# A new order of the unit's steps and of the opening in a 4-bit feed-forward kernel on one core

## The chip, the cores and the metric

One NeuronCore of a Trainium2 chip. Times are device microseconds of one execution of the whole kernel. Five engines run their own instruction streams and meet at semaphores: TensorE (PE, matmuls; PEld is its weight loading), VectorE (DVE), ScalarE (ACT), GpSimd (POOL) and SyncE (SP, which issues the DMAs).

## The reference

For `x` of 4 x 512 x 512 in float32 the kernel computes

```
xn  = layernorm(x)                              # over the last axis
y   = causal_convolution(xn, K) + D * xn        # K: a kernel of 512 taps from the S4 parameters
g, u = xn @ Wg.T, xn @ Wu.T                     # Wg, Wu: 1792 x 512
out = x + y + (silu(g) * u) @ Wd.T              # Wd: 512 x 1792
W   = NF4_CODE[q] * absmax                      # each weight: a 4-bit code, one scale per 64 codes
```

There are 2048 tokens (16 tiles of 128), 512 features and 1792 inner features (14 tiles of 128, `NM`). All three weight matrices come as int32 codes and block scales and have to be turned into numbers on the chip.

## The kernel before

**Numbers.** Each float32 operand of a matmul is split in two float16 halves, high and low, and each product is three matmuls (high by high, high by low, low by high).

**Units.** A unit is a 128 x 512 tile of weights; there are 42: gate and up of each of the 14 inner tiles, and 14 of the down matrix. Making one takes: the codes by DMA; `first_pass` on POOL (line 845) for one side of the code table, and a chain of six passes on ACT (line 936); on DVE `step(u, WHOLE)` (line 1309), which joins the sides, and `step(u, SCALED)` (line 1313), which multiplies by the scales; the high half, `weight_hi(u)`, on ACT (line 963) for the first seven units and on POOL (line 858) from the eighth on; the low half, `weight_lo(u)`, on DVE (line 1323), which waits for the high half. Behind `SCALED` of an up unit DVE makes two sums for the blocked products (`up_sums`, lines 1347 and 1349), POOL copies a gate unit (`gate_copy`, line 867), and DVE makes two more sums (`other_sums`, lines 1357 and 1360), whose halves are `block_hi` on ACT (1057) and `block_lo` on DVE (1369, 1372).

**Stages.** 1. The opening (to about 33 us): the norms of the x tiles (`stats`, `moments`, `rstd` in twelve small steps on DVE; the normalising on ACT for tile 0 and on POOL, line 749, for the others), the common scales (`scales`), the transposes of tiles 0 to 7 on PE (`turn`, line 2145), their halves (`x_hi` on ACT, line 1095; `x_lo` on DVE, line 1551), and the first products (line 2109). 2. Gate and up products of inner tiles 0 to 2 for all four token groups of 512, in the order of `OPENING`. 3. A window for each inner tile from 3 to 13. Windows 3 and 4 are mixed; from 5 on both halves of the tokens go by a scheme with seven block products instead of eight, `blocked_product` (line 2264), for each of two sides s. On PE a window is: product 1 of both sides, product 4 of the tile before, then 5, 6, 2, 3 and 7 of both sides. DVE adds them up in joins (line 1412): product 3 waits for the side's first join, product 4 for its second. The output of gate and up goes through silu on ACT (line 1020), a multiplication on DVE (`h_mul`, line 1438), and the halves of h (`h_hi`, on POOL line 827, and `h_lo`, line 1450). 4. The convolution as Toeplitz matmuls (line 2331), from about 297 us; the down products (lines 2341 and 2391) to the end. The S4 kernel's own small steps (line 1798 and around) lie between the items of windows 7, 8 and 10 to 13 as a `stage` called behind each slot.

**What sets the order.** Each engine's list is written out by hand. In a window the items of the units (three for each unit on DVE) are dealt over eight slots by `eighths`: with two units per window slots 1, 2, 3 and 5, 6, 7 hold one item each, with three units slots 0 to 6 hold one each and slot 7 two. `EARLY_IN` says which inner tiles' windows make a down unit as well as their two, so that they have three; the last window, 13, has three in any case. From window 6 on `window(k)` on DVE runs: second join, `h_mul(n + 3)`, second join of the other side, `h_mul(n + 1)`, `block_lo(k, 1)`, `h_mul(n + 2)`, slots 0 and 1, `h_mul(n)`, slots 2 and 3, the first join of side 0, slot 4, `h_lo`, slot 5, the first join of side 1, slots 6 and 7, `other_sums(k + 1)`, `block_lo(k + 1, 0)`. On ACT, `copy_m1(1, k)` (line 1029) waits for `h_mul(n)`, and side 1's product 6 for that copy. On POOL each unit u from 7 on is, in this order: `first_pass(u + 2)`, which waits for `step(u, WHOLE)`; `h_hi` of the tile before, if u is a window's first unit; `weight_hi(u)`, which waits for `step(u, SCALED)`; `gate_copy(u)`.

In the opening PE runs two groups of matmuls with the identity whose results nothing reads (`warm_up`, line 2130): ten before the first transpose of x and six behind the fourth.

## Time and profile before

| | |
|---|---|
| time, median of 3 runs | 459.99 us (459.29 to 460.63) |
| the profiled execution: time, span | 460.08 us, 458.3 us |
| PE matmul busy | 438.2 us (96%), 2560 matmuls |
| PE weight load busy | 248.8 us (54%) |
| DVE busy | 398.4 us (87%) |
| ACT busy | 278.8 us (61%) |
| POOL busy | 214.6 us (47%) |
| chain that ended last | PE 85%, DVE 6%, ACT 2%, issue 2%, DMA 2%, POOL 1% |

An engine's busy time is what its instructions cover; overlapping instructions of one engine count once. A row of a timeline gives the start, the length, the engine, the line, what is written and read, how many instructions it merges, and in brackets how long the engine stood before it and what it waited for. The length is that of one instruction from its start to its end; in a dense row the next one starts some 0.08 us before the last one's end, so a DVE step of 0.68 takes 0.60 of the engine's time.

### The profile page before, as it was taken

How to read it: one execution, taken by the hardware profiler on the slowest of the kernel's cores; microseconds unless marked ns; L12 is line 12 of the kernel's file. 1: busy time of each engine (PE TensorE's matmuls, PEld its weight loads, DVE VectorE, ACT ScalarE, POOL GpSimd, SP SyncE). 2: the span in 40 equal slices, each digit the busy share in tenths (PEclk: the TensorE clock that was granted, in tenths of full speed). 3: DMA queues.
4: the chain of work that ended last, by engine and by line, in shares of the span. 5: the costliest groups of instructions: out<-in, count | busy, mean ns of one | idle time of the engine just before them, and what ended most of it. 6: DMA issues, size and time to landing. Idle time of an engine off the chain costs nothing.

```text
span 458.3 us, 7272 instructions
## 1 busy us (share of the span) xinstructions
PE 438.2 (96%) x2560; PEld 248.8 (54%) x2560; DVE 398.4 (87%) x641; ACT 278.8 (61%) x472; POOL 214.6 (47%) x163
## 2 busy tenths in 40 slices
PE   1879999999999999999999999999999999999997
PEld 1534444443444444434444444466544788888886
DVE  5988979969889798999897879879996999999993
ACT  7868594295877759588684787856032542445340
POOL 2777299547456848669646847778100000000000
PEclk9989999999999999999999999999999999999999
DMA  8543636022315415155222233457691021101111
GB/s 291 172 131 139 144 75 182 1 92 71 138 47 183 161 47 200 54 183 191 63 69 65 61 80 101 111 187 249 193 369 60 1 94 47 46 1 48 47 47 46
DMA packets 34168, 51.41 MB, mean 112 GB/s; under 512 B 13076, under 2 KB 14164, under 8 KB 33364
## 3 DMA queue, kind: packets, MB, share of 16 engines
q1 hardware_dynamic: 34132, 50.95, 35.3%
q8 instruction: 20, 0.33, 0.3%
q14 instruction: 16, 0.13, 0.1%
HBM read 38.03 MB, written 10.81 MB: 107 GB/s over the span
## 4 chain that ended last, share of the span: by engine, by line
PE 85%; DVE 6%; ACT 2%; issue 2%; DMA 2%; POOL 1%; SPq 0%; DVEq 0%; ACTq 0%; POOLq 0%
PE bank L2264 33%; PE bank L2391 21%; PE bank L2109 16%; PE bank L2341 8%; PE bank L2331 6%; ACT work L936 1%; DMA h<-in_x 1%; DVE h L1438 1%; DVE work L1313 1%; DMA work<-in_q_gate 1%; DVE w L1323 1%; DVE work L1309 1%; PE bank L2145 0%; DVE h L1412 0%; POOL h L845 0%
## 5 line engine op out<-in xcount | busy, mean ns | idle before, releaser
L936 ACT ACTIVATE work<-work 128x512 f32<-128x512 f32 (+1 forms) x234 | 130.0, 628 | 11.5 <-POOL work L845 7.8
L845 POOL TENSOR_SCALAR work<-work 128x512 f32<-128x512 int32 x39 | 85.9, 2202 | 64.4 <-DVE work L1309 46.1
L2264 PE MATMUL bank<-h 128*128 128x512 f16 x360 | 81.5, 379 | 0.9 <-ACT bank L1029 0.9
L2109 PE MATMUL bank<-xT,w 128*128 128x512 f16 (+1 forms) x300 | 66.2, 377 | 2.3 <-DVE w L1323 1.1
L2264 PEld LDWEIGHTS bank<-h 128*128 128x128 f16 x360 | 34.9, 98 | 44.0 <-ACT bank L1029 2.4
L2391 PE MATMUL bank<-wd,work 128*128 128x256 f16 x504 | 56.2, 273 | 0.0
L2264 PE MATMUL bank<-xT,w 128*128 128x512 f16 x240 | 55.4, 379 | 0.0
L2391 PEld LDWEIGHTS bank<-wd,work 128*128 128x128 f16 (+1 forms) x504 | 49.3, 98 | 6.0
L2109 PEld LDWEIGHTS bank<-xT,w 128*128 128x128 f16 x300 | 29.4, 99 | 36.8 <-DVE w L1323 2.4
L1250 ACT ACTIVATE work<-h 128x896 f16<-128x896 f32 x30 | 27.9, 942 | 28.4 <-DVE h L2017 18.3
L2391 PE MATMUL bank<-h,work 128*128 128x256 f16 x378 | 42.2, 273 | 0.0
L858 POOL TENSOR_SCALAR w<-work,sc 128x512 f16<-128x512 f32 x21 | 39.0, 1857 | 6.6 <-DVE work L1313 5.6
L2391 PEld LDWEIGHTS bank<-h,work 128*128 128x128 f16 x378 | 37.0, 98 | 4.3
L2264 PEld LDWEIGHTS bank<-xT,w 128*128 128x128 f16 x240 | 23.4, 98 | 28.1
L2341 PE MATMUL bank<-wd,h 128*128 128x512 f16 x168 | 36.4, 379 | 0.0
L1309 DVE SCALAR_TENSOR_TENSOR work<-work 128x512 f32<-128x512 f32 x39 | 28.4, 729 | 5.1 <-ACT work L936 5.1
L2003 DVE TENSOR_TENSOR work<-h,work 128x896 bf16<-128x896 f32 x30 | 32.5, 1083 | 0.1
L1313 DVE SCALAR_TENSOR_TENSOR work<-work 128x512 f32<-128x512 f32 x41 | 29.9, 730 | 1.5
L1029 ACT ACTIVATE bank<-bank 128x512 f32<-128x512 f32 x20 | 11.6, 582 | 31.7 <-DVE work L1438 15.6
L1020 ACT ACTIVATE work<-bank,sc 128x512 f32<-128x512 f32 x36 | 24.6, 684 | 9.9 <-PE bank L2109 9.9
L2264 PE MATMUL bank<-xT,h 128*128 128x512 f16 x120 | 28.1, 379 | 1.2 <-DVE bank L1412 1.0
L858 POOL TENSOR_SCALAR wd<-work,sc 128x512 f16<-128x512 f32 x14 | 26.3, 1877 | 4.7 <-DVE work L1313 3.8
(181 smaller groups left out, 672.0 us busy)
## 6 DMA issues: line engine op xcount, KB each, us to landing
moved<-h SPq DMA_DIRECT2D x6, 1024.0 KB, 4.9
h<-moved SPq DMA_DIRECT2D x4, 1536.0 KB, 15.5
h<-in_x SPq DMA_DIRECT2D x8, 512.0 KB, 5.4
xT<-in_x SPq DMA_DIRECT2D x16, 256.0 KB, 3.5
out<-xT SPq DMA_DIRECT2D x15, 256.0 KB, 2.1
work<-in_q_gate SPq DMA_DIRECT2D x14, 256.0 KB, 3.6
work<-in_q_up SPq DMA_DIRECT2D x14, 256.0 KB, 2.9
work<-in_am_gate SPq DMA_DIRECT2D x28, 128.0 KB, 3.1
```

Of the source, the lines that this page charges most:

```text
L845: pool.tensor_scalar(chain_room(u, "r"), qs[:, u % 2, :], RIGHT_FROM, RIGHT_FROM, ALU.max, ALU.subtract).then_inc(first_done, 1)
L858: pool.tensor_scalar(weight_of(u)[HI], whole_of(u), scale_of(u), None, ALU.mult).then_inc(phi_done, 1)
L936: nc.scalar.activation(room, qs[:, u % 2, :] if j == 0 else room, KNEE, scale=scale, bias=bias, alpha=below).then_inc(knee_done, 1)
L1250: nc.scalar.activation(slot_of(o)[:, HI], src, ACT.Copy).then_inc(o_hi, 1)
L1309: ins = v.scalar_tensor_tensor(whole, left, CHAIN_TOP if u in CHAINED else LEFT_TOP, right, ALU.min, ALU.add)
L1313: ins = v.scalar_tensor_tensor(whole, whole, CHAIN_STEP if u in CHAINED else -LEFT_TOP, am[:, u % 2, :], ALU.add, ALU.mult)
L2003: v.tensor_tensor(slot[:, LO].bitcast(BF16), src, slot[:, HI], ALU.subtract).then_inc(o_lo, 1)
L2109: mm = nc.tensor.matmul(out_b, weights(k)[:, unit, wl, f, :], xT[:, TPC * c + first:TPC * c + last, xl, f, :], start=(i == 0), stop=(i == ...
L2264: mm = nc.tensor.matmul(out_b, weight(wl, f), token(xl, f), start=(n == 0 and i in (1, 5)), stop=(n == 5), skip_group_check=i not in (1, 5))
L2331: mm = nc.tensor.matmul(bank[(t + 4) % 8][:, P * j:HD], xT[:, t, xl, j, :], tz[:, tl, 0:HD - P * j], start=(n == 0), stop=(n == 3 * NC - 1))
L2341: mm = nc.tensor.matmul(bank[(t + 4) % 8][:], part, wd[:, mt, wl, :], start=(mt == 0 and n == 0), stop=(mt == NM - 1 and n == 2))
L2391: mm = nc.tensor.matmul(out_b, part, w, start=(n == 0), stop=(n == 3 * KT - 1))
```

## The change

Six edits. (1) `EARLY_IN` goes from (7, 8, 9, 11) to (6, 7, 9, 12). (2) On DVE each unit's three items come in the order low half of the unit before, whole, scaled; before it was whole, scaled, low half of the unit before. (3) In the windows from 6 on `h_mul(n)` comes behind slot 0 instead of behind slot 1. (4) The two groups of unread identity products are gone, and the product that spreads the common scales comes ahead of `turn(0)`. (5) In the opening the steps of the norms, scales, first units and transposes come in another order on SP, POOL, ACT, DVE and PE. (6) On PE `products(1, (0,))` comes ahead of `turn(4)`. The same work is done otherwise.

```diff
--- before.py
+++ after.py
@@ -119,7 +119,7 @@
 
 
 
-EARLY_IN = (7, 8, 9, 11)
+EARLY_IN = (6, 7, 9, 12)
 EARLY = len(EARLY_IN)
 SEQ = list(range(9))
 for k in range(3, NM - 1):
@@ -662,11 +662,11 @@
             load_x(1)
             load_codes(1, q_up[0])
             sp.dma_start(amf, am_flat).then_inc(amf_ld, 16)
-            load_x(2)
-            load_x(3)
             load_absmax(0, am_gate[0])
             load_codes(2, q_gate[1])
+            load_x(2)
             load_absmax(1, am_up[0])
+            load_x(3)
             load_codes(3, q_up[1])
             load_absmax(2, am_gate[1])
             sp.dma_start(cols[:], s4_cols).then_inc(s4_ld, 16)
@@ -871,9 +871,9 @@
                 norm(t)
             first_pass(2)
             first_pass(3)
-            first_pass(4)
             for t in range(TPC, 2 * TPC):
                 norm(t)
+            first_pass(4)
             first_pass(5)
             for i in range(14):
                 v_step(i)
@@ -1100,10 +1100,10 @@
             chain(1, 0, 5)
             norm(0)
             chain(1, 5, 6)
+            chain(2, 0, 1)
+            weight_hi(0)
             x_hi(0)
-            weight_hi(0)
             x_hi(1)
-            chain(2, 0, 1)
             x_hi(2)
             x_hi(3)
             chain(2, 1, 2)
@@ -1111,17 +1111,16 @@
             chain(2, 2, 6)
             chain(3, 0, 2)
             weight_hi(2)
-            chain(3, 2, 4)
+            chain(3, 2, 6)
+            silu(0)
+            act.wait_ge(b_mm, 1)
+            nc.scalar.activation(yv[:, 0:2], bank[3][:, 0:2], ACT.Copy).then_inc(b_cp, 1)
+            weight_hi(3)
             x_hi(4)
-            chain(3, 4, 6)
-            silu(0)
-            chain(4, 0, 1)
-            weight_hi(3)
             x_hi(5)
             x_hi(6)
-            act.wait_ge(b_mm, 1)
-            nc.scalar.activation(yv[:, 0:2], bank[3][:, 0:2], ACT.Copy).then_inc(b_cp, 1)
             x_hi(7)
+            chain(4, 0, 1)
             chain(4, 1, 6)
             h_hi(0)
             silu(1)
@@ -1327,7 +1326,7 @@
                 for p in range(first, last):
                     u, i = item_of(DVE_AT, p)
                     if u in CHAINED:
-                        i = (3, 4, 2)[i]
+                        i = (2, 3, 4)[i]
                     if i != 2:
                         step(u, i if i < 2 else i - 1)
                     elif u > 0:
@@ -1566,27 +1565,27 @@
             rstd(0, 3)
             rstd(0, 4)
             rstd(0, 5)
-            step(0, WHOLE)
+            scales(1)
             rstd(0, 6)
             rstd(0, 7)
             rstd(0, 8)
-            scales(1)
+            scales(2)
             rstd(0, 9)
-            scales(2)
+            scales(3)
             rstd(0, 10)
-            scales(3)
+            scales(4)
             rstd(0, 11)
-            scales(4)
             dve.wait_ge(id_done, 1)
             scales(5)
+            scales(6)
+            step(0, WHOLE)
+            step(0, SCALED)
             stats(4)
-            scales(6)
-            step(0, SCALED)
-            step(1, WHOLE)
             scales(7)
             scales(8)
+            step(1, WHOLE)
+            weight_lo(0)
             x_lo(0)
-            weight_lo(0)
             x_lo(1)
             step(1, SCALED)
             x_lo(2)
@@ -1596,31 +1595,31 @@
             stats(6)
             stats(7)
             moments(4, 8)
+            step(2, WHOLE)
             rstd(1, 0)
             rstd(1, 1)
             rstd(1, 2)
-            scales(9)
+            step(2, SCALED)
             rstd(1, 3)
             rstd(1, 4)
             rstd(1, 5)
-            step(2, WHOLE)
+            scales(9)
             rstd(1, 6)
             rstd(1, 7)
             rstd(1, 8)
-            step(2, SCALED)
+            weight_lo(2)
             rstd(1, 9)
+            scales(10)
             rstd(1, 10)
+            scales(11)
             rstd(1, 11)
-            weight_lo(2)
             stats(8)
-            x_lo(4)
-            scales(10)
             step(3, WHOLE)
-            scales(11)
+            scales(12)
             step(3, SCALED)
             h_mul(0)
-            scales(12)
             weight_lo(3)
+            x_lo(4)
             x_lo(5)
             x_lo(6)
             stats(9)
@@ -1763,9 +1762,9 @@
                     h_mul(n + 1)
                     block_lo(k, 1)
                     h_mul(n + 2)
-                    stage_of(0, 2)
+                    stage_of(0, 1)
                     h_mul(n)
-                    stage_of(2, 4)
+                    stage_of(1, 4)
                     join(0, k, 0)
                     stage_of(4, 5)
                     h_lo(n)
@@ -2145,15 +2144,14 @@
                     mm = nc.tensor.transpose(bank[4 + t % TPC][:, P * f:P * f + P], xnb[:, t, P * f:P * f + P], ident[:])
                 mm.then_inc(tp_done, 1)
 
-            warm_up(10)
-            turn(0)
             pe.wait_ge(one_done, 1)
             pe.wait_ge(sc_done, 7)
             nc.tensor.matmul(bank[0][:, P:P + 6], ones[:], dg3, start=True, stop=True).then_inc(mx_bc, 1)
+            turn(0)
             turn(1)
             turn(2)
             turn(3)
-            warm_up(6)
+
 
             pe.wait_ge(wlo_done, 1)
             pe.wait_ge(xlo_done, 2)
@@ -2165,8 +2163,8 @@
             for i in range(2):
                 mm = nc.tensor.matmul(bank[3][:, i:i + 1], vcs[:, P * i:P * i + P], bps, start=True, stop=True)
             mm.then_inc(b_mm, 1)
+            products(1, (0,))
             turn(4)
-            products(1, (0,))
             turn(5)
             turn(6)
             turn(7)
```

## Rows read from the trace of the kernel before

**Rows 1.** The page: the span, and the x loads among the DMA issues

```profile
span 458.3 us, 7272 instructions
...
h<-in_x SPq DMA_DIRECT2D x8, 512.0 KB, 5.4
```

**Rows 2.** Waits of TensorE: engine, line, releaser: total us, times, longest

```profile
PE bank L2145 <- POOL h L749: 2.9, 1, 2.9
PE bank L2109 <- DVE w L1323: 1.1, 1, 1.1
PE bank L2264 <- DVE bank L1412: 1.0, 1, 1.0
PE bank L2264 <- ACT bank L1029: 0.9, 1, 0.9
```

**Rows 3.** Timeline, TensorE, 0 to 40: start, us, engine line op out<-in xcount

```profile
9.81 2.34 PE L2130 MATMUL bank<-ident 128*128 128x256 f16 x10
...
17.13 1.47 PE L2109 MATMUL bank<-xT,w 128*128 128x256 f16 x12 [0.62 <-DVE xT L1551]
...
26.88 4.45 PE L2109 MATMUL bank<-xT,w 128*128 128x512 f16 x12
...
33.01 7.30 PE L2109 MATMUL bank<-xT,w 128*128 128x512 f16 x33 [0.37 <-ACT yv L1123]
```

**Rows 4.** Busy time by stretch: five engines, then the granted clock, DMA, GB/s

```profile
28.00:32.00 4.00, 4.00 (x17) 1.95 (x16) 3.56 (x8) 2.79 (x6) 3.23 (x3) 0.66 0.00 1
```

**Rows 5.** Timeline, VectorE, 0 to 60, the same columns

```profile
25.74 1.09 DVE L1323 SCALAR_TENSOR_TENSOR w<-work,sc,w 128x512 f16<-128x512 f32 x1 [0.32 <-ACT w L963]
...
34.24 0.68 DVE L1551 TENSOR_TENSOR xT<-bank,xT 128x512 f16<-128x512 f32 x1
...
47.62 0.73 DVE L1323 SCALAR_TENSOR_TENSOR h<-work,sc,h 128x512 f16<-128x512 f32 x1
```

**Rows 6.** Timeline, ScalarE, 0 to 60

```profile
24.98 0.72 ACT L963 ACTIVATE w<-work,sc 128x512 f16<-128x512 f32 x1 [3.10 <-DVE work L1313]
...
33.31 3.15 ACT L936 ACTIVATE h<-h 128x512 f32<-128x512 f32 x5
```

**Rows 7.** Timeline, GpSimd, 0 to 70

```profile
25.52 3.45 POOL L749 TENSOR_SCALAR h<-h 128x512 f32<-128x512 f32 x4 [1.40 <-DVE h L1544]
```

**Rows 8.** Timeline, VectorE, 60 to 130

```profile
110.80 1.09 DVE L1323 SCALAR_TENSOR_TENSOR w<-work,sc,w 128x512 f16<-128x512 f32 x1
```

**Rows 9.** Timeline, VectorE, 200 to 300, in tile 9's and tile 11's windows

```profile
205.11 0.68 DVE L1309 SCALAR_TENSOR_TENSOR work<-work 128x512 f32<-128x512 f32 x1
...
207.26 0.47 DVE L1349 SCALAR_TENSOR_TENSOR h<-work,sc,h 128x256 f32<-128x256 f32 x1
...
211.80 1.09 DVE L1323 SCALAR_TENSOR_TENSOR w<-work,sc,w 128x512 f16<-128x512 f32 x1
...
251.76 0.75 DVE L1323 SCALAR_TENSOR_TENSOR w<-work,sc,w 128x512 f16<-128x512 f32 x1 [1.39 <-POOL w L858]
```

**Rows 10.** Timeline, GpSimd, 200 to 300, first unit of tile 10's window

```profile
224.72 1.93 POOL L845 TENSOR_SCALAR work<-work 128x512 f32<-128x512 int32 x1 [3.41 <-DVE work L1309]
226.71 0.61 POOL L827 CAST h<-work 128x512 f16<-128x512 f32 x1
227.29 2.01 POOL L858 TENSOR_SCALAR w<-work,sc 128x512 f16<-128x512 f32 x1
```

**Rows 11.** Timeline, TensorE, 130 to 200: first products of tile 6, its product 3

```profile
143.04 2.75 PE L2264 MATMUL bank<-xT,w 128*128 128x512 f16 x12
...
155.99 2.75 PE L2264 MATMUL bank<-xT,h 128*128 128x512 f16 x12
```

**Rows 12.** Timeline, VectorE, 130 to 200: the first join in tile 6's window

```profile
144.59 0.68 DVE L1412 TENSOR_TENSOR h<-bank,h 128x512 f32<-128x512 f32 x1
```

**Rows 13.** Timeline, VectorE, 200 to 300, in tile 13's window

```profile
289.22 0.91 DVE L1798 TENSOR_SCALAR wd<-wd,sc 128x512 f16<-128x512 f32 x1
...
294.40 0.69 DVE L1412 TENSOR_TENSOR h<-bank,h 128x512 f32<-128x512 f32 x1 [0.60 <-PE bank L2264]
```

## The prediction

> **What bounds the kernel now.** I read the busy times first: TensorE (PE) is busy nearly throughout the 458.3 us span [rows 1]. Then its waits [rows 2], leaving out the 9.7 us before its first instruction, which the change doesn't shorten: 2.9 us in the opening, 1.1 us on a low half (line 1323) at the end of tile 3's window, and 1.0 and 0.9 us in tile 8's window, on a join and on the copy behind the last `h_mul`. Everywhere else PE sets the pace. A wait that goes is gained whole if no other takes its place; a delay of VectorE (DVE) costs nothing until it eats the slack before the product that asks for its result. Third, the timelines of DVE and GpSimd (POOL), for that slack.
>
> **The opening.** The 16 unread identity products go: ten take 2.34 us [rows 3], all in waits, so they free no time on the critical path. `step(0, WHOLE)` (0.6) leaves the chain of small steps, but the first product still waits for `weight_lo(0)`, then two `x_lo`: by my count of the new order 17.0 against 17.13 [rows 3]. No gain there.
> The second tile's gate product is where the order bites. It now starts at 26.88, behind `turn(4)`; its low half, begun at 25.74 [rows 5], had waited for ScalarE (ACT), which had stood 3.1 us for `step(2, SCALED)` [rows 6]. In the new order DVE ends the moments at 21.6, W(2) at 22.2, three small steps at 22.6, S(2) at 23.2; ACT's high half takes 0.7, and the low half runs 24.3 to 25.0. (W, S, L: the whole, scaled and low-half steps of a unit.) The product doesn't wait for a transpose any more and starts at 25.0, 1.9 earlier. Its twelve matmuls took 4.45 us [rows 3], with a granted clock of 0.66 over 28 to 32 [rows 4], the lower level (1.2 GHz) for most of it, after a wait of 2.9. Twelve at the upper level take 2.6 (0.216 each in the dense stretches). The idle time ahead of it is now 1.6 at most, so I take 2.6: end 27.6. The norms of x tiles 4 to 7 still start with the last small step, at 25.6 against 25.52 [rows 7], and end 29.1; the last transpose is done 29.7, `products(1, (1,))` 32.3, and the last `x_lo`, now at 34.24 [rows 5], ends at 32.4. Products of the third pair start at 32.4 against 35.6 (33.01 [rows 3] and twelve of 0.216): 3.2 earlier.
> Not all of it lasts. Fifteen products later PE asks for the low half of unit 5: now at 48.5, when that half (47.62 plus 0.73) is just done [rows 5]. ACT's fourth chain, now over at 36.46 [rows 6], ends at 34.4 (`x_hi(7)` at 30.6 and six passes of 0.63), and DVE is behind it all the way, so unit 5 is ready 2.2 earlier. I count **-2.3**.
> SP: x tiles 4 to 7 go behind two scale loads and the codes of unit 2, whose issue waits for the first knees (5.4); with 5.4 us to land [rows 1] and a start near 6.1 the first is there at 11.6, and `stats(4)` asks at 13. It costs nothing; a late one would delay the scales, and with them all weights, by as much. The other moves of POOL (`first_pass(4)` behind the norms, ends 31.0, first asked for at 32.5) and ACT cost nothing either.
>
> **Tile 3's window.** L(9), now last [rows 8], comes right behind the second join, so PE's 1.1 us wait [rows 2] goes: **-1.1**. In tile 4's window the next low half waits for POOL some 1.6 us, inside DVE's own wait of 1.2 for PE and a join slack of 1.7: 0.
>
> **The blocked windows.** Before, a unit's three items come as W(u), S(u), L(u-1); after, as L(u-1), W(u), S(u). So L(u) follows S(u) as the next item, where W(u+1) and S(u+1) had lain between. L(u) needs the high half from POOL, and POOL's queue behind W(u) is `first_pass(u+2)`, 1.93, then `h_hi` 0.61 at a window's first unit, then `weight_hi(u)`, 2.01, 1.6 with DVE quiet [rows 10]: from the end of W(u) to the high half **4.4** us at a first unit, 3.9 at a second. DVE has between them at a first unit in a three-unit window only S (0.7) and the two sums (0.9): W 205.11 to the end of the sums at 207.7 [rows 9]. It stands 2.8 us. At the second unit `h_lo`, S and a join (1.9) lie between: 2.0 more. Before, the same distance held five or more items (W 205.11, the window's first unit's L at 211.8) and cost nothing; where POOL was late, in tile 11's window, L already stood 1.39 [rows 9].
> Behind the stalled L wait, on DVE, the two first joins of the window, and PE's product 3 waits for these. With P as the window's start on PE, product 3 of one side comes at P+12.95 (143.04 to 155.99 [rows 11]), of the other 1.3 later. **Tile 6**, now with three units: DVE starts its first join at P+1.55 [rows 12], is through the three `h_mul` and L(u-1) at P+7.3, W 7.9, sums 9.5; high half 12.4, L 13.0, join 13.65: PE stands 0.75. W, `h_lo`, S, second join 16.1 against 14.25+0.75: 1.15 more. **+1.9**. The third unit ends DVE's window at P+21.5, that is 1.5 after PE's next start, as it entered.
> **Tile 7** the same with 1.7 us of inverse steps in it: joins at P+14.35 and 17.5, PE stands 1.4 and 1.85, less the 0.4 it loses now: **+2.9**. **Tile 8** loses its third unit, and `h_mul(n)` comes before W; both waits there [rows 2] go but 0.3: **-1.7**. **Tile 9** (three units before and after) enters with 1.8 us more slack: **+0.7**. Tiles 10 and 11 have other work of theirs in the gap: 0. **Tile 12** gets a third unit: **+0.7**, and ends 2.8 after PE's start, so PE's product 4 stands **1.0**. **Tile 13**, three units and the kernel's scaling (two steps, the first at 289.22 [rows 13], 1.6 in all): stalls of 3 and 2 us, joins 0.4 and 1.5 late; then DVE comes to the last two joins at P+23.0, 2.1 behind product 7, where now it stands 0.60 for PE [rows 13], and product 4 waits for them: **+4.0**. In the convolution and behind it DVE stalls again (1.0 per unit), which the 4 us of waits for loads and for ACT there cover.
> Sum of the windows +1.9 +2.9 -1.7 +0.7 +0.7 +1.0 +4.0 = +9.5. With -2.3 and -1.1: **+6.1**. The profiled execution took 460.08, 1.8 around its span of 458.3, and the median is 459.99, so they stand for each other: 466.
> Bounds: the high half costs DVE at least nothing (L finds it ready) and at most 4.1 less the 1.6 between, at each unit; VectorE beside a busy POOL stretches single steps from 0.7 to 1.1 [rows 5, 8], which adds up to 0.7 per three-unit window, some 4 in all.
>
> **A rule against the opening's part.** The identity products are also the only long run of ordinary matmuls before 17.13: the first ten ran at 0.234 per 256 columns, the pace of the lower level, and the first product's twelve at 0.123, the upper [rows 3]. What is left before it are transposes. By the Trainium skill ("TensorE: Matmul & The Clock Gate", Part 4: PE-mode transpose) a transpose doesn't count as busy in the same way for the clock. By that rule the rival below on the clock holds; no row here parts transposes from matmuls.
>
> **Rivals.** *DVE has the room (faster).* L finds its high half, or the stalls fit into DVE's idle time. POOL would have to deliver within 1.6 us of W instead of 4.4, or a three-unit window would need 5 us idle on DVE; now they have 1 to 2. For it speak the two-unit windows, with 2.5 us idle, that steps beside a quiet POOL run in 0.7 instead of 1.1, and that the early units leave tile 8, where PE stood. It decides below some 1 us of stall per unit. Then -2.3 -1.1 -2.0 = -5.4: 454.6; with half of the stalls about 460.
> *The clock (slower still).* The first 36 matmuls run at the lower level throughout: 24 of 0.213 and 12 of 0.427 are 10.2 instead of 5.2. They end near 27.9, the next gate product at 30.7, the third pair starts at 35.0: the opening gives 0.6 instead of 2.3, 468. Against it: the transposes fill the time from 12 to 16, and PE has 1.6 us to spare before 25.0.
> *It does nothing.* Gains and stalls cancel: tile 13's last joins cost 1 instead of 4 and the rest 0.5 each; 460.
>
> **Chances.** My forecast 0.53, the clock on top of it 0.09, room on DVE 0.28, nothing 0.10. A measurement of this kernel can tell about 0.3% from no change. Slower 0.62, same 0.09, faster 0.29. The forecast's own range is 462 to 471 (opening -3 to -1, tile 13 +1.5 to +5, port contention up to +4); with the other side it is 455 to 471.
>
> **What would show it.** Right: in the rows after, line 1323 of DVE with waits for POOL of 2 to 3 us in the windows of tiles 6, 7, 9, 12 and 13; PE waits for joins (line 1412) of 8 us or more in all; product 4 of tile 13 late; no wait at 111; the third pair's start at 32 to 33. Wrong: DVE waits for POOL under 1 us each, or PE dense from 33 to 297; or a granted clock at the lower level between 17 and 33, and the opening no shorter.

## The result and the profile after

The changed kernel takes 477.15 us (475.77 to 477.67), the one before 459.64 beside it: a ratio of 1.0377 (95% interval 1.0344 to 1.041), or 17.5 us slower where 6.1 were forecast. The profiled execution has a span of 475.6 us against 458.3 [rows 1], so it has the same difference, 17.3. Lines of the changed kernel are one or two lower than before: W is 1308, S 1312, L 1322, the join 1411, the fourth product of the epilogue 1437.

The page after: the span, busy times, and the chain that ended last.

```profile
span 475.6 us, 7240 instructions
...
PE 439.3 (92%) x2544; PEld 247.2 (52%) x2544; DVE 395.3 (83%) x641; ACT 281.9 (59%) x472; POOL 209.0 (44%) x163
...
PE 58%; DVE 18%; POOL 7%; issue 7%; DMA 5%; ACT 3%; SPq 0%; DVEq 0%; POOLq 0%; ACTq 0%
```

The engines have about the same to do and are busy for a smaller share. The chain was PE for 85% before and is PE for 58% now, with 25% on DVE and POOL (7% before). The waits, of PE, DVE, POOL and ACT (engine, line, releaser: total us, times, longest; against [rows 2]):

```profile
PE bank L2262 <- DVE bank L1411: 11.9, 9, 2.1
...
PE bank L2262 <- DVE h L1411: 3.8, 3, 1.6
...
PE bank L2262 <- DVE h L1368: 0.8, 1, 0.8
```

```profile
DVE wd L1322 <- POOL wd L858: 19.1, 10, 3.3
DVE w L1322 <- POOL w L858: 16.2, 7, 2.9
```

```profile
POOL work L845 <- DVE work L1308: 82.6, 29, 5.8
```

```profile
ACT work L936 <- POOL work L845: 26.2, 19, 1.9
```

L now waits for POOL's high half 17 times, 35.3 us in all; before it did so for 3.3. POOL's `first_pass` in turn waits 82.6 us for W, where it waited 46.1. Two engines that each wait for the other, and neither is full: they take turns. One turn, in tile 7's window, on DVE (172.01 on) and on POOL:

```profile
172.01 0.68 DVE L1308 SCALAR_TENSOR_TENSOR work<-work 128x512 f32<-128x512 f32 x1
...
172.87 0.68 DVE L1312 SCALAR_TENSOR_TENSOR work<-work 128x512 f32<-128x512 f32 x1
173.68 0.62 DVE L1346 TENSOR_TENSOR h<-work 128x256 f32<-128x256 f32 x1
174.22 0.47 DVE L1348 SCALAR_TENSOR_TENSOR h<-work,sc,h 128x256 f32<-128x256 f32 x1
177.59 0.75 DVE L1322 SCALAR_TENSOR_TENSOR w<-work,sc,w 128x512 f16<-128x512 f32 x1 [2.90 <-POOL w L858]
...
179.26 0.68 DVE L1308 SCALAR_TENSOR_TENSOR work<-work 128x512 f32<-128x512 f32 x1
```

```profile
172.84 2.50 POOL L845 TENSOR_SCALAR work<-work 128x512 f32<-128x512 int32 x1 [3.28 <-DVE work L1308]
175.40 0.61 POOL L827 CAST h<-work 128x512 f16<-128x512 f32 x1
175.99 1.57 POOL L858 TENSOR_SCALAR w<-work,sc 128x512 f16<-128x512 f32 x1
180.10 2.23 POOL L845 TENSOR_SCALAR work<-work 128x512 f32<-128x512 int32 x1 [2.54 <-DVE work L1308]
```

W(u) ends at 172.7, POOL needs until 177.56, L(u) stands 2.90 for it, and only behind L comes W(u+1), at 179.26; by then POOL has stood 2.54. The joins lie behind these L: product 3 of tile 7 starts after waits of 1.75 and 2.07 on PE.

Where the 17.3 us lie, from the starts of each window on PE in the two timelines (us; the third column is the window after minus before):

| stretch | before | after | more | forecast |
|---|---|---|---|---|
| to tile 3's start (PE's first instruction came at 9.54 after, 9.65 before) | 87.41 | 86.29 | -1.1 | -2.3 |
| from there to the product that waited for L(9) | 24.54 | 23.31 | -1.2 | -1.1 |
| from there to tile 5's start | 15.55 | 15.54 | 0 | 0 |
| tile 5 | 15.54 | 16.62 | +1.1 | 0 |
| tile 6 | 18.13 | 22.75 | +4.6 | +1.9 |
| tile 7 | 18.49 | 24.02 | +5.5 | +2.9 |
| tile 8 | 20.45 | 19.07 | -1.4 | -1.7 |
| tile 9 | 18.13 | 19.81 | +1.7 | +0.7 |
| tiles 10, 11 | 39.04 | 39.04 | 0 | 0 |
| tile 12 | 18.27 | 19.40 | +1.1 | +0.7 |
| tile 13 | 21.24 | 26.84 | +5.6 | +5.0 |
| convolution | 26.08 | 26.08 | 0 | 0 |
| first part of the down products (line 2339) | 36.26 | 37.66 | +1.4 | 0 |

### The profile page after: what moved, and what is told of

Its sections match the earlier page's. It is cut to its first block, busy times and chain, and to the rows that moved or that the text cites. A ratio compares the mean times of both kernels' runs of the same rounds, so it can differ in the third digit from the quotient of the medians.

```text
span 475.6 us, 7240 instructions
## 1 busy us (share of the span) xinstructions
PE 439.3 (92%) x2544; PEld 247.2 (52%) x2544; DVE 395.3 (83%) x641; ACT 281.9 (59%) x472; POOL 209.0 (44%) x163
## 4 chain that ended last, share of the span: by engine, by line
PE 58%; DVE 18%; POOL 7%; issue 7%; DMA 5%; ACT 3%; SPq 0%; DVEq 0%; POOLq 0%; ACTq 0%
PE bank L2389 20%; PE bank L2262 15%; PE bank L2108 10%; PE bank L2339 7%; PE bank L2329 5%; POOL work L845 3%; DVE work L1308 3%; DMA lines<-wd 3%; DVE work L1312 2%; POOL w L858 2%; DVE w L1322 2%; DVE bank L1411 2%; DVE h L1498 1%; ACT work L936 1%; DMA h<-in_x 1%
## 5 line engine op out<-in xcount | busy, mean ns | idle before, releaser
L936 ACT ACTIVATE work<-work 128x512 f32<-128x512 f32 (+1 forms) x234 | 131.7, 623 | 36.7 <-POOL work L845 26.2
L845 POOL TENSOR_SCALAR work<-work 128x512 f32<-128x512 int32 x39 | 87.3, 2238 | 92.5 <-DVE work L1308 82.6
L2108 PE MATMUL bank<-xT,w 128*128 128x512 f16 (+1 forms) x300 | 64.7, 371 | 3.8 <-DVE w L1322 1.9
L2262 PE MATMUL bank<-xT,h 128*128 128x512 f16 x120 | 29.8, 390 | 11.9 <-DVE bank L1411 11.9
L858 POOL TENSOR_SCALAR w<-work,sc 128x512 f16<-128x512 f32 x21 | 36.0, 1716 | 7.2 <-DVE work L1312 6.0
L1322 DVE SCALAR_TENSOR_TENSOR w<-work,sc,w 128x512 f16<-128x512 f32 x25 | 20.2, 808 | 16.4 <-POOL w L858 16.2
L1312 DVE SCALAR_TENSOR_TENSOR work<-work 128x512 f32<-128x512 f32 x41 | 30.8, 752 | 2.2
L2262 PE MATMUL bank<-h,w 128*128 128x512 f16 x120 | 28.0, 379 | 3.8 <-DVE h L1411 3.8
```

The source lines that it names most:

```text
L845: pool.tensor_scalar(chain_room(u, "r"), qs[:, u % 2, :], RIGHT_FROM, RIGHT_FROM, ALU.max, ALU.subtract).then_inc(first_done, 1)
L858: pool.tensor_scalar(weight_of(u)[HI], whole_of(u), scale_of(u), None, ALU.mult).then_inc(phi_done, 1)
L936: nc.scalar.activation(room, qs[:, u % 2, :] if j == 0 else room, KNEE, scale=scale, bias=bias, alpha=below).then_inc(knee_done, 1)
L1312: ins = v.scalar_tensor_tensor(whole, whole, CHAIN_STEP if u in CHAINED else -LEFT_TOP, am[:, u % 2, :], ALU.add, ALU.mult)
L1322: v.scalar_tensor_tensor(lo, whole_of(u), scale_of(u), hi, ALU.mult, ALU.subtract).then_inc(wlo_done, 1)
L2108: mm = nc.tensor.matmul(out_b, weights(k)[:, unit, wl, f, :], xT[:, TPC * c + first:TPC * c + last, xl, f, :], start=(i == 0), stop=(i == ...
```

## The experiments

Each is given against the kernel before or the changed kernel, and its ratio is to the kernel before, run beside it (459.3 to 459.9 us). In each W, S and L are as in the prediction.

**The parts one by one.** e1: the changed kernel with the old order of a unit's items.

```diff
-                        i = (2, 3, 4)[i]
+                        i = (3, 4, 2)[i]
```

> The changed kernel with the unit's three items back in their old order (whole, scaled, low half of the unit before); the early tiles, the opening, the missing identity products and the earlier h_mul(n) stay. If the new order is the cause of the loss: no waits of VectorE's low half for GpSimd of 2.9 us, nearly no PE waits between 33 and 297 us, and the gains stand alone: 1.1 us measured at the start of tile 3's window and the 1.9 us of tile 8's window, 456 to 458 us, ratio 0.991 to 0.996. If instead the missing identity products, the opening or the new early tiles carry a good part of the loss: above 463 us.

Measured 460.01, ratio 1.0008 (0.9995 to 1.002). L(9) waits its 1.07 again; everything else of the 17 us is gone. e2: the kernel before with the new order alone (the same line the other way).

> The kernel before with one edit: the unit's three items in the new order. If the order is the cause: tile windows 7, 8, 9, 11 and 13 have three units, each stands 2.9 us and 1.9 us at its two low halves; PE loses some 5 us in tile 7, 4 in tile 8 (it had lost 2 before), 1.7 in tile 9, 1 in tile 11, 5.5 in tile 13 and 2 in tile 5, less 1.1 in tile 3: 474 to 480 us. If the order costs only together with the new early tiles: under 466 us.

Measured 471.43, ratio 1.0255 (1.023 to 1.0279): less than I expected. So the order is necessary for the loss, but two thirds of it by itself. e3: the kernel before with the opening's order on all engines and without the identity products; e4: only `EARLY_IN = (6, 7, 9, 12)`.

> The kernel before with the new orders of the opening on all engines and without the identity products; nothing changed in the windows. The changed kernel began tile 3's window 1.1 us earlier. If this gain carries to the end: 458.9 us, ratio 0.9975, third pair of products at 33.7 us. If the windows' own loops take it back: 460 us. If cold matmuls eat it: a granted clock under 1 between 17 and 33 us, and no gain.

> The kernel before with EARLY_IN (6, 7, 9, 12) alone. Under my theory tile 8's window loses its third unit and with it both PE waits (1.9 us), and tiles 6 and 12 have room for one in the old order: 458 us, ratio 0.996, no PE wait in tile 6's window above 0.5 us. Rival: the third unit in tile 6 costs what the one in tile 8 did: 460 us.

Measured: e3 459.08, 0.9981 (0.9966 to 0.9996), a gain of 0.9; e4 460.21, 1.0021 (1.0002 to 1.0039), a loss of 1.0. Both are small: their intervals end just short of no change. In e4 PE waits 0.79 in tile 6, which now has a third unit, and 0.72 in tile 7, which had one before too; both waits are for ACT's bank copy (line 1029), and tile 8's join wait stays at 1.00. These three parts by themselves add up to 11.8, and with the fourth (e10, below) to 13.7, not 17.5, so some of them meet. e7 has order and places together, e9 the changed kernel with `h_mul(n)` back behind slot 1, e10 the move of `h_mul(n)` alone in the kernel before (the "moved product" is this step on DVE):

```diff
-                    stage_of(0, 1)
+                    stage_of(0, 2)
                     h_mul(n)
-                    stage_of(1, 4)
+                    stage_of(2, 4)
```

> The kernel before with two of the four parts: the new order of the items of each unit, and the down units at tiles 6, 7, 9, 12. The order alone cost 11.6 us and the other places alone 1.0, while all parts together cost 17. Theory 1 (the parts meet at these places: two three-unit windows in a row, 6 and 7, with no slack carried between, and a third unit in tile 12 whose lateness tile 13 takes over): 475 to 478 us, with 4.5 or more lost in each of the windows 6 and 7 and 5 in 13. Theory 2 (the meeting is with the opening's new order or the moved product of the epilogue): 471 to 473 us.

> The changed kernel with one part taken back: the epilogue's fourth product (h_mul(n)) stands after the items of the first two eighths of a window again, not after those of the first. Two of the four parts together (order and places of the down units) took 471.2 us, all four 477. Theory 1: the moved product puts the first unit's W or S, and with them GpSimd's halves, one product (0.7 us) later, so the L wait of a window is 2.90 us where it was 2.05, and each three-unit window costs about 1 us more: without it 470.0 to 471.5 us, the first L wait of tile 7 at 2.0 to 2.1 us. Theory 2: it is the opening's order that meets the rest: 476 to 477.5 us.

> The kernel before with only the moved product (h_mul(n) after the first eighth's items). Theory 1 (it costs only where GpSimd's halves are already what L waits for, which in the old order they are not): 459.3 to 460.2 us, ratio 0.999 to 1.002. Theory 2 (it takes about 0.7 us from the second join of each window by itself): 461 to 464 us.

Measured: e7 471.16, 1.0259 (1.023 to 1.0289), the same as the order alone: it is not the places, whose 1.0 us by themselves doesn't show on top of the order. e9 471.70, 1.0256 (1.0229 to 1.0283), against 1.0377 with the moved product: it costs 1.2% or 5.6 us here, where e10 has 1.9. e10 461.75, 1.0042 (1.0025 to 1.0059): 1.9 us in the old order, my second theory: PE's waits for joins are 3.4 us in all against 1.0 [rows 2], in tiles 7, 8, 10 and 11. ACT's wait in tile 8 (0.9) is gone in return. With the product ahead of slot 1, in which W or S of the window's first unit lies, that step comes 0.7 later and POOL's halves with it. In the new order L then stands 2.90 in tile 7, where in e7 and e9 it stands 2.05. Windows 6, 7, 9 and 12 are 21.6, 23.0, 18.6 and 18.2 long in e9 and 22.8, 24.0, 19.8 and 19.4 in the changed kernel: 1.1 to 1.2 in each. The row of e7 (VectorE, tile 7's first unit):

```profile
175.09 0.75 DVE L1323 SCALAR_TENSOR_TENSOR w<-work,sc,w 128x512 f16<-128x512 f32 x1 [2.05 <-POOL w L858]
```

**Is it POOL?** e5: the changed kernel with a shorter `first_pass` from tile 5's units on (7/8 of that side's decoding is left out). e13: the same cut in the kernel before.

```diff
-                pool.tensor_scalar(chain_room(u, "r"), qs[:, u % 2, :], RIGHT_FROM, ...
+                n = CH if u < made_before(5) else 64
+                pool.tensor_scalar(chain_room(u, "r")[:, 0:n], qs[:, u % 2, 0:n], RIGHT_FROM, ...
```

> The changed kernel, with VectorE's new order, in which GpSimd's subtraction of the right half (first_pass) takes 64 of its 512 columns from the fifth tile's units on. The part left out is the decoding of 448 columns of those units, so its time is that of a smaller computation. Theory 1: L(u) waits for GpSimd's two halves of the unit (up to 3.3 us in the changed kernel, 35.3 us in 17 waits), and that wait is what became late for TensorE. With first_pass 1.3 to 1.7 us shorter each wait shrinks by about as much: 35 us of L waits fall to 10 or less, the unit that VectorE finishes last in a window comes in time, and the kernel takes 461 to 468 us. Theory 2: VectorE has simply too much to do in three-unit windows, and its order only moves the place where that shows: L waits fall and the joins wait instead, 473 to 477 us.

> The kernel before, with the same cut as e5_pass_cut: GpSimd's subtraction of the right half takes 64 of 512 columns from the fifth tile's units on; what is left out is the decoding of the other 448 columns. Theory 1 (in the old order L waits 3.3 us for GpSimd in the whole run, so a shorter subtraction gives TensorE nothing): 458 to 460 us, and the 15 us that the cut gave the changed kernel are the order's. Theory 2 (GpSimd's amount of work is a bound of its own): 450 us or less.

Measured: e5 462.08, 1.0063 (1.0042 to 1.0084), 15 us below the changed kernel. e13 459.31, 0.9994 (0.9982 to 1.0005). The same cut gives 15 us in the new order and nothing in the old. So POOL's amount of work is no bound; how soon it delivers is what costs, and only in the new order. Two waits shrink at once in e5, so it doesn't part them: ACT's chain waits 2.3 us for `first_pass` instead of 26.2, and L's waits are:

```profile
DVE wd L1323 <- POOL wd L859: 11.0, 10, 1.8
DVE w L1323 <- POOL w L859: 9.0, 6, 1.7
```

20.0 instead of 35.3 us in all, not the 10 that I expected; with each under 1.9 the joins are nearly in time (PE waits 4.6 us for them instead of 15.7). e6: POOL makes the high half first.

```diff
-                if u + 2 < UNITS:
+                late = u >= made_before(6)
+                if not late and u + 2 < UNITS:
                     first_pass(u + 2)
 ...
                 weight_hi(u)
+                if late and u + 2 < UNITS:
+                    first_pass(u + 2)
```

> The changed kernel, in which GpSimd makes the high half of a unit's weight ahead of the subtraction for the unit two later, for the units from tile 6 on. Theory 1 (L waits for the high half, because it stands behind that subtraction on GpSimd): L waits fall from 2.9 us to 1.2 or less; the subtraction comes about 1.5 us later, and ScalarE's chain, which waits for it, comes later by as much. If ScalarE has the room, 464 to 469 us; if its chain is what then ends last, 474 to 480 us. Theory 2 (VectorE's amount of work alone): 474 to 477 us whatever GpSimd's order.

Measured 475.81, 1.0349 (1.0318 to 1.0381). L's waits fall to 15.7 us (1.7 at most), yet the time stays. The waits of DVE and of ACT in e6:

```profile
DVE h L1371 <- ACT h L1060: 17.8, 8, 3.2
DVE wd L1325 <- POOL wd L858: 8.6, 9, 1.1
```

```profile
ACT work L939 <- POOL work L845: 52.0, 22, 5.3
```

ACT's chain now waits 52.0 us for the late `first_pass` (26.2 before this edit), and `block_lo` 17.8 for ACT. Both of POOL's steps hang on the late W: whichever goes first, someone stands.

**Which exchange?** The new order moves L(u-1) ahead of both W(u) and S(u). e14: the kernel before with L between the two. e16: the changed kernel with the same.

```diff
-                        i = (3, 4, 2)[i]
+                        i = (3, 2, 4)[i]
```

> The kernel before with a third order of a unit's items, W(u), L(u-1), S(u): L stands ahead of S only. Old order (W, S, L) 459.7 us; new order (L, W, S) 471.4. W(u) starts ScalarE's next step and the subtraction two units later; S(u) releases GpSimd's high half. Theory 1 (L's wait costs by how many of the unit's items stand between it and the high half of the unit before, and by how late W and S leave): L(u-1) comes after S(u-1) and W(u) only, its waits are about 0.7 us shorter than in the new order (27 to 30 us in all become 15 to 20), and W(u) isn't late: 463 to 467 us. Theory 2 (what costs is that S(u), and so the high half, comes late): 469 to 472 us. Theory 3 (only W's place matters): 459.5 to 461 us.

> The changed kernel with one exchange: W(u), L(u-1), S(u) in place of L(u-1), W(u), S(u). Theory 1 (the 17 us are W(u)'s place behind L's wait, and the moved product and the places of the down units cost only through it): 458.5 to 460.5 us, L's waits for GpSimd under 10 us in all. Theory 2 (the moved product and two three-unit windows in a row, 6 and 7, cost in this order too, by 2 to 5 us): 461 to 465 us.

Measured: e14 458.03, 0.9973 (0.9958 to 0.9988), faster than any of my three theories allowed, and 13 us faster than e2, from which it differs by the exchange of two neighbouring items, W(u) and L(u-1). L waits for POOL 5.1 us in all (3.6 for gate and up units, 1.5 for down units; 3.3 before), and PE waits 2.2 for joins. The rows of VectorE in tile 7's window, to hold beside those of the changed kernel:

```profile
164.53 0.68 DVE L1309 SCALAR_TENSOR_TENSOR work<-work 128x512 f32<-128x512 f32 x1
...
167.07 0.68 DVE L1313 SCALAR_TENSOR_TENSOR work<-work 128x512 f32<-128x512 f32 x1
...
169.37 0.68 DVE L1309 SCALAR_TENSOR_TENSOR work<-work 128x512 f32<-128x512 f32 x1
...
170.97 0.73 DVE L1323 SCALAR_TENSOR_TENSOR w<-work,sc,w 128x512 f16<-128x512 f32 x1
```

W(u) starts at 164.53, W(u+1) at 169.37 without waiting for anything of POOL's, and L(u), at 170.97, finds its half done: 5.8 us lie between W(u)'s end and L(u), more than the 4.8 that POOL took here. In the changed kernel W(u+1) stands behind L(u), so this distance can't grow. Why S behind L is even a gain is told by the waits of PE: L(9)'s 1.07 and ACT's 0.95 in tile 8 are gone, at 0.55 and 0.6 more at joins (tiles 7 and 8). That is 0.9 net, of the 1.2 measured (0.6 to 1.9 by the interval).

e16 462.24, 1.0045 (1.0021 to 1.0069): 15 of the 17.5 us come back by this exchange alone. By themselves the moved product (+1.9), the places (+1.0), the opening (-0.9) and e14's order (-1.2) would come to +0.8 and not the 2.1 measured (1.0 to 3.2 by the interval). In its profiled execution one L wait of 5.40 us stands out, and PE's 2.05 behind it; tile 13 is 25.1 long there, 21.2 before. POOL's rows say what made it long:

```profile
272.06 1.94 POOL L845 TENSOR_SCALAR work<-work 128x512 f32<-128x512 int32 x1 [4.96 <-DMA work<-in_q_down]
274.09 1.57 POOL L858 TENSOR_SCALAR wd<-work,sc 128x512 f16<-128x512 f32 x1
```

The high half stood behind a `first_pass` that waited 4.96 for the codes of a down unit. The kernel before has such a wait too (5.34, at 274.23), but no L that waits behind it. So in this execution nearly the whole difference to the kernel before lies in tile 13, behind a load, and how the prices of the four parts add up can't be read from it.

**The opening and the identity.** e11: the kernel before without its sixteen unread products.

```diff
-            warm_up(10)
 ...
-            warm_up(6)
```

> The kernel before without the ten and the six unread products of the identity, nothing else changed. The products' twelve 256-column matmuls then follow sixteen transposes alone. Theory 1 (TensorE is held by the values of the rows there, and its granted clock is at the upper level without them as it was in the changed kernel: 0.123 us for each of the 12 matmuls of 256 columns): 459.3 to 460.0 us, ratio 0.999 to 1.001. Theory 2 (transposes don't raise the clock, and the first products run at 0.234 us each like the first ten identity products): the first 12 at 2.8 us instead of 1.5, 460.9 to 462 us.

Measured 460.35, 1.001 (0.9992 to 1.0028): no difference. TensorE's timeline of e11, behind sixteen transposes alone:

```profile
17.60 1.47 PE L2109 MATMUL bank<-xT,w 128*128 128x256 f16 x12 [0.41 <-DVE xT L1551]
...
26.75 0.66 PE L2145 MATMUL bank<-ident,h 128*128 128x128 f32 x4 [2.43 <-POOL h L749]
27.30 4.45 PE L2109 MATMUL bank<-xT,w 128*128 128x512 f16 x12
```

The twelve of 256 columns take 1.47, 0.123 each, the pace that they had with the identity ahead of them [rows 3]. It isn't so in every execution. Eleven profiled kernels have no identity products; in seven the first twelve take 1.47, in four (e5, e6, e8, e12) the first 36 matmuls take 6.7 to 7.5 together, where the changed kernel's take 5.8. e8:

```profile
13.33 3.68 PE L2144 MATMUL bank<-ident,h 128*128 128x128 f32 x16
18.36 6.73 PE L2108 MATMUL bank<-xT,w 128*128 128x256 f16 x36 [1.35 <-DVE xT L1550]
25.92 2.76 PE L2108 MATMUL bank<-xT,w 128*128 128x512 f16 x12 [0.31 <-DVE w L1322]
```

The first six there take 1.44, about what twelve take at the upper level. With the identity, all seven profiled kernels start at the upper pace; one execution of each is too few to say that the identity does it. The microsecond is taken up by a wait that follows: from the first transpose to the gate product e8 needs 12.59 us, the changed kernel 12.60 (it waited 1.25 where e8 waits 0.31). So either pace comes out about the same here, as the ratio of e11 says too.

**A version that beats both.** e8: the kernel before with the opening, and the new order for units 9 and 10 only. e12: the same with `EARLY_IN = (7, 9, 11, 12)`. e15: the opening with e14's order.

```diff
-                        i = (3, 4, 2)[i]
+                        i = (3, 4, 2)[i] if u >= made_before(4) else (2, 3, 4)[i]
```

> The kernel before with the opening of the change, and the new order of the items only for the two units of the first blocked tile (9 and 10). L(9) then comes ahead of W(10) and S(10), and tile 3's 1.07 us of waiting goes, as it went in the change. Theory 1 (the order costs only where GpSimd's halves are late, in windows with three units and in those behind them): opening 0.9 and tile 3 1.0 to 1.2 add up, 457.4 to 458.2 us, ratio about 0.995 to 0.997. Theory 2 (VectorE gives it back at the joins of tiles 5 and 6): 459 us, ratio 0.998 to 1.0.

> The kernel of e8_first_units (opening of the change, new order for units 9 and 10 only; 457.6 us) with the down units at tiles 7, 9, 11, 12 instead of 7, 8, 9, 11. Tile 8, where TensorE waits 0.95 for ScalarE's bank and 1.03 for VectorE's join, then has two units. Theory 1 (ScalarE's wait there goes, the join's stays, as it did with two units in tile 8 before; tiles 11 and 12 have the room): 456.6 to 457.2 us. Theory 2 (two three-unit windows in a row at 11 and 12 cost what two in a row at 6 and 7 did, 0.7 each): 457.5 to 458.5 us.

> The kernel before with the opening of the change and the third order of a unit's items, W(u), L(u-1), S(u). The third order alone took 458.0 us (1.07 us of waiting in tile 3 gone, 0.95 in tile 8 gone, the join of tile 8 0.6 later, 0.55 new in tile 7), the opening alone 459.1, or 0.9 below its kernel of before. Theory 1 (they are in different stretches and add up): 456.8 to 457.4 us, ratio 0.994 to 0.996. Theory 2 (the opening's microsecond is taken up by tile 3 to 8, where VectorE then stands later against TensorE): 457.8 to 458.3 us.

Measured: e8 457.59, 0.9963 (0.9947 to 0.9979); e15 458.06, 0.9962 (0.9948 to 0.9976); e12 460.31, 1.0017 (0.9997 to 1.0036). e8 and e15 beat the kernel before by 0.4% (1.7 us) and can't be told apart; their gain is also not told from e14's 0.3%, so whether the opening's 0.9 adds to e14's is open. e12 is unexplained: its profiled execution has a span of 456.2 us, past the opening PE waits of 1.00 and 0.84 only, and is the shortest of twelve, whose median is 2.3 above it. No view of one execution shows what the others lost. A candidate, not tested, is the load that e16 shows: e12's twelve times spread over 5.1 us (458.0 to 463.1), e16's ten over 6.1, and even in e12's shortest POOL waits 1.67 for a down unit's codes at 268.28 and S 0.85 for its scales at 270.29.

## Why the prediction was wrong

The direction and the mechanism were right, and the size was off by a factor of nearly three: 466 was forecast, 477.2 measured, outside the range. What failed is the sum over the windows: +9.5 was forecast for them and nothing for the rest behind tile 3, and they cost +18.2 and +1.4. The steps that failed are the path that I put at nothing (from a late W over ACT's chain into the next window), the 4.4 us from W to the high half, the price of a wait on PE, and the clock inside a window.

**Right.** L's stall: 2.8 and 2.0 were forecast for the first and second unit; 2.91 and 1.86 were measured in tile 6, 2.90 and 1.14 in tile 7, 2.90 and 1.86 in tile 9. Tile 3's wait goes (-1.2 for -1.1). Tile 8 gets faster (-1.4 for -1.7), tiles 10 and 11 don't change, tile 13 costs 5.6 for 5.0: its waits on PE are 0.80, 0.79, 1.62 and 1.56, forecast as 1.0, 0.4, 1.5 and 2.1. PE's waits for joins, "8 us or more", are 15.7.

**Tiles 5 to 7, the largest miss (+11.2 for +4.8).**

```profile
126.96 0.63 ACT L936 ACTIVATE work<-work 128x512 f32<-128x512 f32 x1 [1.49 <-POOL work L845]
```

```profile
128.66 1.67 PE L2262 MATMUL bank<-h 128*128 128x512 f16 x7 [0.76 <-DVE h L1368]
...
145.92 2.87 PE L2262 MATMUL bank<-h,w 128*128 128x512 f16 x12 [1.40 <-DVE h L1411]
...
157.80 1.47 PE L2262 MATMUL bank<-xT,h 128*128 128x512 f16 x6 [1.25 <-DVE bank L1411]
160.62 1.47 PE L2262 MATMUL bank<-xT,h 128*128 128x512 f16 x6 [1.35 <-DVE bank L1411]
```

- The path that the sum put at nothing. It has 0 for tile 4 and no term for tile 5. W one item later makes `first_pass` later, and ACT's chain waits for it (1.49 at 126.96). So `block_hi` was late, PE stood 0.76 in tile 5, and the L before tile 6 stood 1.48; tile 5's second join, the first step of tile 6's window, was late and PE stood another 1.40 at 145.92. I had followed POOL's lateness into DVE only, never into ACT. In e2, which has the order alone, the same two waits are there (0.76 and 1.40), so they are the order's.
- The 4.4 us from W to the high half. They were 4.8 in tile 6 and 4.9 in tile 7, because `first_pass` took 2.43 and 2.50 where I had 1.93. The two waits behind it are 2.60 for 1.9 in tile 6 and 3.82 for 3.25 in tile 7.
- The price of a wait. A product behind a wait starts some 0.16 later than the wait accounts for: from 141.76 to 145.92 are 4.16, with a wait of 1.40 and 2.59 for the twelve matmuls before it. Tiles 5 to 13 have thirteen such waits, 2 us that the sum lacks.
- The clock in tile 7 (below), some 1.7. I had weighed the clock for the opening alone.

The moved product is in the sum, but without a price of its own: it is part of "the three `h_mul` and L(u-1) at P+7.3", and the stall of 2.8 is the one with it (2.07 in e9). By e9 and the changed kernel it costs 5.6 us. Without it tiles 6 and 7 would still cost +3.5 and +4.5, more than was forecast with it.

**Tile 9 (+1.7 for +0.7) and 12 (+1.1 for +0.7).** The forecast gave tile 9 more slack on entering and each of the two 0.7. Without the moved product (e9) tile 9 costs 0.5 and tile 12 nothing; with it DVE comes later by more than that slack.

**The down products (+1.4 for 0).** That "the 4 us of waits for loads and for ACT there cover" DVE's stalls was wrong. L stands 1.81 three times between 327 and 338 and 1.03 at 343.08, DVE's steps at line 1959 come late, and PE waits 0.9 for them.

**The opening (-1.1 for -2.3).** The gate product starts at 25.28 and takes 2.76, as worked out (25.0 and 2.6 without the tail of the pipeline). But the third pair starts at 33.7 and not 32.4, because of DVE's steps beside POOL's norms:

```profile
26.77 1.08 DVE L1308 SCALAR_TENSOR_TENSOR work<-h 128x512 f32<-128x512 f32 x1 [0.48 <-ACT h L936]
...
27.96 1.08 DVE L1312 SCALAR_TENSOR_TENSOR work<-work 128x512 f32<-128x512 f32 x1
...
29.83 1.09 DVE L1322 SCALAR_TENSOR_TENSOR w<-work,sc,w 128x512 f16<-128x512 f32 x1
```

Three steps at 1.08 where I had put 0.7: L(3) ends at 30.8 and TensorE's next product starts at 31.07, against a forecast of 29.7 for `turn(7)`'s end. I had rows of both lengths [rows 5, 8] and used the longer for the range alone. DVE stays that much behind: L(5) is done at 47.4, forecast at 46.1, and PE stands 0.34 for it. In e7, where the opening is missing, and e9, where it isn't, the ratios are the same (1.0259 and 1.0256), but each is known to 1.3 us only, so whether its 0.9 is kept on top of the new order is open.

**The rivals.** "DVE has the room" fell with the 17 waits. "The clock" fell for this execution: the first 36 matmuls ran at the upper level, the twelve of the next gate product too (granted clock 1.00 over 24 to 32, where it was 0.66 over 28 to 32 [rows 4]). For the first products the row lengths say it, not the column: it shows 1.00 from the start, also while the first transposes take 0.22 each and later ones 0.12:

```profile
12.68 3.59 PE L2144 MATMUL bank<-ident,h 128*128 128x128 f32 x16
17.71 1.47 PE L2108 MATMUL bank<-xT,w 128*128 128x256 f16 x12 [1.44 <-DVE xT L1550]
...
25.28 2.76 PE L2108 MATMUL bank<-xT,w 128*128 128x512 f16 x12 [1.25 <-DVE w L1322]
27.88 1.47 PE L2144 MATMUL bank<-ident,h 128*128 128x128 f32 x12
```

Sixteen transposes and an idle 1.44 us, and ahead of them one small transpose and two products of six columns, were all that came before 17.71. The rule that I had weighed (the Trainium skill, "TensorE: Matmul & The Clock Gate", Part 4: PE-mode transpose) would have put them at the lower pace. This trace, e11's and five others (1.47 for the first twelve) don't agree with that; the four with 6.7 to 7.5 for the first 36 do, in part. What parts them isn't known. Even there the rival's price was wrong. It had all 36 at the lower level, 5 us more and 1.7 of them lost for good; in those four the 36 take 0.9 to 1.7 more, and the gate product starts 12.6 to 13.0 us behind the first transpose, against 12.6 in the changed kernel.

## What to carry to other kernels

When two engines hand a unit back and forth, look at what stands behind the waiting step in its queue: if it is the step that feeds the other engine with the next unit, the pipeline becomes a loop, and each unit costs both engines' times one after the other. Exchanging two neighbouring items (W(u) ahead of L(u-1)) was worth 13 us here, with no work taken away, and the busy shares hardly tell the orders apart (DVE 83% and POOL 44% of the span in the changed kernel, 87% and 47% before); the waits do. And price every moved step by what it delays on the other engines, each of them in turn, not only on the one that you are following; a 0.7 us step that cost 1.9 us over the whole kernel in the old order cost 5.6 in the new one, 1.1 to 1.2 in each of four windows.

## What the runs showed of the hardware

**The clock falls behind waits of some 2 us, but not behind each.** In tile 7 of the changed kernel, TensorE's timeline, then the busy time by stretch (its length, PE's busy time, the granted clock, DMA share, GB/s):

```profile
179.41 1.47 PE L2262 MATMUL bank<-xT,h 128*128 128x512 f16 x6 [1.75 <-DVE bank L1411]
182.95 2.42 PE L2262 MATMUL bank<-xT,h 128*128 128x512 f16 x6 [2.07 <-DVE bank L1411]
185.16 3.53 PE L2262 MATMUL bank<-h 128*128 128x512 f16 x12
```

```profile
183.00:185.00 2.00, 2.00 (x6) 0.58 0.87 319
185.00:187.00 2.00, 2.00 (x6) 0.57 0.99 328
```

Six matmuls take 2.42 instead of 1.47, and twelve 3.53 instead of 2.75: 1.7 us, beside the 3.8 of waiting. Behind waits of 1.09 and 2.01 us in e2 (at 196.9 and 200.38) the clock stayed at the upper level; in the opening it stayed so behind 2.23 (e14) and fell behind 2.43 (e11, the row at 27.30 above). In e7 it stayed up behind 2.46 in the opening and fell in tile 7 behind waits of 0.62 and 2.07 (granted clock 0.73 over 180 to 182, 0.50 over 182 to 184). Which of the two comes can't be read from the wait's length alone in these rows.

**DVE beside a busy POOL.** In the changed kernel W, S and L (128 x 512 float32) took 0.66 to 0.75 in every row with POOL quiet. Beside POOL many rows are no longer, and fourteen are 1.07 to 1.18; so company of POOL is needed for a long step and doesn't make each one long. It can be POOL that gives way instead: S at 172.87 took 0.68 inside a `first_pass` of 2.50. `first_pass` itself took from 1.92 to 2.81.
